# A fused transformer kernel on one core: value and output products of the first cross attention from 16-bit halves

## What is computed

```python
q = (inputs_q @ Wq).reshape(b, sq, H, HD) * (1.0 / np.sqrt(HD))
k = (inputs_kv @ Wk).reshape(b, skv, H, HD)
v = (inputs_kv @ Wv).reshape(b, skv, H, HD)
scores = jnp.einsum('bqhd,bkhd->bhqk', q, k)
attn = jax.nn.softmax(scores, axis=-1)
ctx = jnp.einsum('bhqk,bkhd->bqhd', attn, v).reshape(b, sq, H * HD)
return ctx @ Wo
```

## Time and profile before

| | |
|---|---|
| median of the runs | 704.66 us |
| the profiled execution | 703.56 us, span of its instructions 702.3 us |
| PE busy | 662.5 us (94%) |
| weight loads busy (beside PE) | 421.8 us (60%) |
| DVE busy | 557.1 us (79%) |
| ACT busy | 379.8 us (54%) |
| POOL busy | 333.7 us (48%) |
| value products (L942), 50 to 420 us | 16.0 us in 104 instructions |
| output products (L948), 50 to 420 us | 14.9 us in 50 instructions |
| last output product of the first attention (L948) | 470.3 us |

### The profile page before, as it was taken

How to read it: one execution, slowest core, us unless ns; L and a number is a source line. 1 busy time by engine, 2 the same in 40 slices (tenths; PEclk the granted TensorE clock), 3 DMA queues, 4 the chain that set the end, 5 groups by cost and what they waited for, 6 DMA issues and landing times. The chain is left out here.

```text
span 702.3 us, 13255 instructions
## 1 busy us (share of the span) xinstructions
PE 662.5 (94%) x4895; PEld 421.8 (60%) x4895; DVE 557.1 (79%) x1000; ACT 379.8 (54%) x610; POOL 333.7 (48%) x449
## 2 busy tenths in 40 slices
PE   9899999999999999999999999996999889887887
PEld 7466766667666776766766666752456444443453
DVE  5997867977787786887988667875897889988655
ACT  5643433334433353443443344445998899898841
POOL 5884444544545416569543316425645543344401
PEclk9999999999999999999999999998999999999999
DMA  9656688565556688987686965519998989998910
GB/s 313 177 125 157 153 171 182 135 150 126 136 129 136 143 181 221 195 204 165 167 182 126 201 137 131 141 39 265 187 193 156 168 156 192 158 177 152 160 37 8
DMA packets 347152, 111.23 MB, mean 158 GB/s; under 512 B 313544, under 2 KB 344528, under 8 KB 346832
## 3 DMA queue, kind: packets, MB, share of 16 engines
q1 hardware_dynamic: 347088, 110.39, 74.7%
HBM read 32.23 MB, written 0.26 MB: 46 GB/s over the span
## 5 line engine op out<-in xcount | busy, mean ns | idle before, releaser
L919 PE MATMUL psum<-c_nat,eT 128*128 128x256 f16 x1536 | 188.1, 273 | 0.9 <-ACT u_sb L1058 0.9
L1702 DVE TENSOR_REDUCE tops<-psum 128x1 f32<-128x512 f32 x256 | 159.2, 680 | 24.5 <-PE psum L1653 24.2
L1695 ACT ACTIVATE cT<-psum,bias,q_scale 128x1024 f16<-128x1024 f32 x128 | 153.5, 1205 | 26.3 <-PE psum L1653 18.4
L919 PEld LDWEIGHTS psum<-c_nat,eT 128*128 128x128 f16 x1536 | 150.3, 98 | 27.0 <-issue 1.6
L891 PE MATMUL psum<-cT,qk 128*128 128x512 f16 x744 | 165.6, 379 | 0.1
L1653 PE MATMUL psum<-kT,v_space 128*128 128x512 f16 x512 | 140.5, 383 | 15.8 <-DVE tops L1702 9.3
L891 PEld LDWEIGHTS psum<-cT,qk 128*128 128x128 f16 x744 | 72.6, 98 | 82.2 <-issue 1.0
L1096 DVE TENSOR_REDUCE neg_max<-psum 128x1 f32<-128x2048 f32 x32 | 73.3, 2290 | 30.9 <-PE psum L891 30.6
L1653 PEld LDWEIGHTS psum<-kT,v_space 128*128 128x128 f16 x512 | 44.6, 98 | 80.7 <-DVE tops L1702 41.5
L1084 DVE TENSOR_TENSOR e_lo<-e_all,e_hi 128x2048 f16<-128x2048 f32 x32 | 87.5, 2733 | 0.0
L732 ACT ACTIVATE qT<-psum 128x128 f32<-128x128 f32 x32 | 8.9, 279 | 120.4 <-PE psum L714 120.3
(11 more groups left out here) (252 smaller groups left out, 901.4 us busy)
## 6 DMA issues: line engine op xcount, KB each, us to landing
wq_h<-in_L_xattn_Wq SPq DMA_DIRECT2D x32, 128.0 KB, 2.5
wk_h<-in_wkT SPq DMA_DIRECT2D x32, 128.0 KB, 2.6
wv_h<-in_L_xattn_Wv SPq DMA_DIRECT2D x32, 128.0 KB, 2.3
wo_h<-in_L_xattn_Wo SPq DMA_DIRECT2D x32, 128.0 KB, 2.5
mx_land<-in_mx_weights SPq DMA_DIRECT2D x8, 384.0 KB, 3.5
v_space<-in_ctx SPq DMA_DIRECT2D x4, 512.0 KB, 5.7
cT<-in_ctx SPq DMA_DIRECT2D x2, 1024.0 KB, 7.6
c_nat<-in_expert_wT SPq DMA_DIRECT2D x2, 1024.0 KB, 6.4
```

The costliest lines, as they stand in the source:

```text
L919: ins = pe.matmul(u_ps, c.eT[:, v % 2, e_part, j, :], m.c_nat[:, v // H0, c_part, j, :], start=(j, e_part, c_part) == (0, 0, 0), stop=(j, ...
L1695: act.activation(m.y[:, u % 2, q * CHUNK:(q + 1) * CHUNK], m.bank(second_place(u, q), 2), ACT.Exp, bias=m.bias[:, u:u + 1], scale=m.q_scal ...
L1702: dve.tensor_reduce(m.tops[:, n // NB, n % NB:n % NB + 1], m.bank(n % 3), AX.X, ALU.max, negate=True).then_inc(s["q_max"], 1)
```

## The change

The value product reads 16-bit halves of Wv (`wvo_parts`, first half high, second low) and of the transposed u, three products per 128 rows of Wv (`TERMS`: high x high, high x low, low x high), six of 128 columns in all; the output product reads halves of the value product and of Wo, three of 256 columns (`HALVED`: for heads 0 to 28; head 29 keeps the fp32 output product). Wv and Wo of a head now lie beside each other in one tile of 512 columns with two places. ACT copies it to fp16 at the head of unit u = w+4; POOL subtracts the copy from it, right behind L672, in the same unit. The fp32 sum of the halves of u (L660) goes, and the halves have two places. ACT's copy of the value product (L1011) is now the high half, and DVE takes the low one right behind the reciprocal. SP loads the output weights behind the transposes of u, and waits for the split two units back instead of an output product. The last two heads take their weights in the places of the query weights, and their uT_sb lies in the place of qk.

```diff
--- before.py
+++ after.py
@@ -43,6 +43,7 @@
 FP8_UNIT = 2.0 ** -6
 UNITS = B * H0
 TURNED = UNITS - 2
+HALVED = TURNED - 1
 
 UP = 64.0
 E_UP = 1024.0
...
@@ -287,15 +288,16 @@
         self.eT = sb("eT", [P, 2, 2, KTB, P], FP16)
         self.wq_h = sb("wq_h", [P, 2, KD, HD0])
         self.wk_h = sb("wk_h", [P, 2, D])
-        self.wv_h = sb("wv_h", [P, 3, KD, HD0])
-        self.wo_h = sb("wo_h", [P, 3, D])
+        self.wvo_h = sb("wvo_h", [P, 2, 2 * D])
+        self.wvo_parts = sb("wvo_parts", [P, 2, 2 * D], FP16)
         self.qT = sb("qT", [P, P])
         self.qk = sb("qk", [P, 2, 2, KD, P], FP16)
         self.u_sb = sb("u_sb", [P, D])
         self.u_parts = sb("u_parts", [P, 2, D], FP16)
-        self.uT_parts = sb("uT_parts", [P, 2, KD, P], FP16)
-        self.uT_sb = sb("uT_sb", [P, 2, KD, P])
+        self.uT_parts = sb("uT_parts", [P, 2, 2, KD, P], FP16)
+        self.uT_sb = flat(self.qk).bitcast(F32).rearrange("p (a k q) -> p a k q", a=2, k=KD)
         self.oT_sb = sb("oT_sb", [P, P])
+        self.oT_parts = sb("oT_parts", [P, 2, P], FP16)
         self.v_top = sb("v_top", [P, D])
         self.neg_max = sb("neg_max", [P, 2])
         self.row_sum = sb("row_sum", [P, UNITS])
@@ -531,10 +533,19 @@
 
 
 def sp_load_output(sp, c, s, t, u):
-    h, sem = u % H0, s[f"wvo_in{u % 3}"]
-    sp.dma_start(c.wv_h[:, u % 3, :, :], t["L0_xattn_Wv"].rearrange("(k p) n -> p k n", p=P)
+
+    h = u % H0
+    if u < TURNED:
+        values, out, sem = value_weights(c.wvo_h[:, u % 2, :]), c.wvo_h[:, u % 2, D:2 * D], s[f"wvo_in{u % 2}"]
+    else:
+        values, out, sem = c.wq_h[:, u % 2, :, :], c.wk_h[:, u % 2, :], s[f"wqk_in{u % 2}"]
+    sp.dma_start(values, t["L0_xattn_Wv"].rearrange("(k p) n -> p k n", p=P)
                  [:, :, h * HD0:(h + 1) * HD0]).then_inc(sem, 16)
-    sp.dma_start(c.wo_h[:, u % 3, :], t["L0_xattn_Wo"][h * HD0:(h + 1) * HD0, :]).then_inc(sem, 16)
+    sp.dma_start(out, t["L0_xattn_Wo"][h * HD0:(h + 1) * HD0, :]).then_inc(sem, 16)
+
+
+def value_weights(both):
+    return both[:, 0:D].rearrange("p (k n) -> p k n", k=KD)
 
 
 def sp_cross(sp, m, c, d, g, s, t):
@@ -542,10 +553,6 @@
         if u + 3 < UNITS:
             sp.wait_ge(s["qk_mm"], u + 2)
             sp_load_query(sp, c, s, t, u + 3)
-        if 4 <= u <= UNITS + 1:
-            if u > 4:
-                sp.wait_ge(s["head_out"], u - 4)
-            sp_load_output(sp, c, s, t, u - 2)
         if 0 < u <= UNITS:
             v = u - 1
             if v > 1:
@@ -555,6 +562,12 @@
             sp.wait_ge(s["e_lo"], v + 1)
             sp.dma_start_transpose(c.eT[:, v % 2, 1], c.e_lo[:, :]).then_inc(s[f"lo_turned{v % 2}"], 16)
             sp_turn_values(sp, c, s, v - 2)
+        if 4 <= u <= UNITS + 1:
+            if u - 2 < TURNED:
+                sp.wait_ge(s["wvo_parts"], 2 * (u - 3))
+            else:
+                sp.wait_ge(s["qk_mm"], UNITS)
+            sp_load_output(sp, c, s, t, u - 2)
         if 0 < u <= H0:
             for kt in (2 * u - 2, 2 * u - 1):
                 sp.wait_ge(s["k_cut"], kt + 1)
@@ -607,10 +620,10 @@
 
 def sp_turn_values(sp, c, s, v):
     if 0 <= v < TURNED:
-        if v > 0:
-            sp.wait_ge(s["uT_out"], v)
+        if v > 1:
+            sp.wait_ge(s["oT"], v - 1)
         sp.wait_ge(s["u_lo"], v + 1)
-        sp.dma_start_transpose(c.uT_parts.rearrange("p a k q -> p (a k) q"), flat(c.u_parts)).then_inc(
+        sp.dma_start_transpose(c.uT_parts[:, v % 2].rearrange("p a k q -> p (a k) q"), flat(c.u_parts)).then_inc(
             s[f"u_turned{v % 2}"], 16)
 
 
@@ -652,15 +665,6 @@
                            ALU.subtract).then_inc(s["c_lo"], 1)
 
 
-def pool_turned_values(pool, c, s, w):
-    if 0 <= w < TURNED:
-        pool.wait_ge(s[f"u_turned{w % 2}"], 16 * (w // 2 + 1))
-        if w > 1:
-            pool.wait_ge(s["oT"], w - 1)
-        pool.tensor_tensor(flat(c.uT_sb[:, w % 2]), flat(c.uT_parts[:, 0]), flat(c.uT_parts[:, 1]), ALU.add).then_inc(
-            s["uT_out"], 1)
-
-
 def pool_cross(pool, m, c, d, g, s, side):
     full = d.k_full.rearrange("p (h d) -> p h d", h=H1)
     for u in range(UNITS + 3):
@@ -670,6 +674,10 @@
             if w > 0:
                 pool.wait_ge(s[f"u_turned{(w - 1) % 2}"], 16 * ((w - 1) // 2 + 1))
             pool.tensor_tensor(c.u_parts[:, 1, :], c.u_sb[:, :], c.u_parts[:, 0, :], ALU.subtract).then_inc(s["u_lo"], 1)
+        if (turned := turned_due(u)) is not None:
+            pool.wait_ge(s["wvo_parts"], 2 * turned + 1)
+            pool.tensor_tensor(c.wvo_parts[:, 1, :], c.wvo_h[:, turned % 2, :], c.wvo_parts[:, 0, :],
+                               ALU.subtract).then_inc(s["wvo_parts"], 1)
         side.upto(4 * u + 1)
         if u in (1, 2):
             tiles = slice((u - 1) * LATE, u * LATE)
@@ -689,10 +697,6 @@
             pool.tensor_tensor(hi, ints, scale, ALU.mult).then_inc(s["k_pool"], 1)
             pool.wait_ge(s["k_pool"], 2 * kt + 2)
             pool.tensor_tensor(lo, full, hi, ALU.subtract).then_inc(s["k_cut"], 1)
-            if kt % 2 == 0:
-                pool_turned_values(pool, c, s, w)
-        if u >= H0:
-            pool_turned_values(pool, c, s, w)
         side.upto(4 * u + 2)
         if H0 + 2 <= u < H0 + 2 + KT // 4:
             value_round(pool, m, s, 2 * (u - H0 - 2) + 1)
@@ -937,15 +941,38 @@
     def value_product(w):
         if w > 0:
             pe.wait_ge(s["added"], w)
-        pe.wait_ge(s[f"wvo_in{w % 3}"], 32 * (w // 3 + 1))
+        pe.wait_ge(s[f"u_turned{w % 2}"], 16 * (w // 2 + 1))
+        pe.wait_ge(s["wvo_parts"], 2 * w + 2)
         for k in range(KD):
-            ins = pe.matmul(o_ps[:, D:D + P], c.wv_h[:, w % 3, k, :], c.uT_sb[:, w % 2, k, :], start=k == 0,
+            for w_part, u_part in TERMS:
+                ins = pe.matmul(o_ps[:, D:D + P], value_weights(c.wvo_parts[:, w_part, :])[:, k, :],
+                                c.uT_parts[:, w % 2, u_part, k, :], start=(k, w_part, u_part) == (0, 0, 0),
+                                stop=(k, w_part, u_part) == (KD - 1, 1, 0))
+        ins.then_inc(s["oT"], 1)
+
+    def output_product(w):
+        pe.wait_ge(s["oT_out"], w + 1)
+        if w < HALVED:
+            pe.wait_ge(s["oT_lo"], w + 1)
+            for o_part, w_part in TERMS:
+                ins = pe.matmul(o_ps[:, 0:D], c.oT_parts[:, o_part, :], c.wvo_parts[:, w_part, D:2 * D],
+                                start=(o_part, w_part) == (0, 0), stop=(o_part, w_part) == (1, 0))
+        else:
+            ins = pe.matmul(o_ps[:, 0:D], c.oT_sb[:, :], c.wvo_h[:, w % 2, D:2 * D], start=True, stop=True)
+        ins.then_inc(s["head_out"], 1)
+
+    def last_value_product(w):
+        pe.wait_ge(s["uT_copied"], w - TURNED + 1)
+        pe.wait_ge(s["added"], w)
+        pe.wait_ge(s[f"wqk_in{w % 2}"], 32 * (w // 2 + 2))
+        for k in range(KD):
+            ins = pe.matmul(o_ps[:, D:D + P], c.wq_h[:, w % 2, k, :], c.uT_sb[:, w % 2, k, :], start=k == 0,
                             stop=k == KD - 1)
         ins.then_inc(s["oT"], 1)
 
-    def output_product(w):
+    def last_output_product(w):
         pe.wait_ge(s["oT_out"], w + 1)
-        pe.matmul(o_ps[:, 0:D], c.oT_sb[:, :], c.wo_h[:, w % 3, :], start=True, stop=True).then_inc(s["head_out"], 1)
+        pe.matmul(o_ps[:, 0:D], c.oT_sb[:, :], c.wk_h[:, w % 2, :], start=True, stop=True).then_inc(s["head_out"], 1)
 
     for u in range(UNITS + 3):
         v = u - 2
@@ -966,7 +993,6 @@
         side.upto(4 * u + 1)
         w, last = turned_due(u), last_due(u)
         if w is not None:
-            pe.wait_ge(s["uT_out"], w + 1)
             value_product(w)
             if last is not None:
                 output_product(w)
@@ -983,8 +1009,7 @@
         drain(u, 2)
         side.upto(4 * u + 3)
         if last is not None:
-            pe.wait_ge(s["uT_copied"], last - TURNED + 1)
-            value_product(last)
+            last_value_product(last)
         elif w is not None:
             output_product(w)
         if u < H0:
@@ -998,7 +1023,7 @@
             ins.then_inc(s["v_scale_pe"], 1)
         drain(u, 3)
         if last is not None:
-            output_product(last)
+            last_output_product(last)
 
 
 def act_cross(act, m, c, s, side):
@@ -1008,7 +1033,7 @@
         act.wait_ge(s["oT"], w + 1)
         if w > 0:
             act.wait_ge(s["head_out"], w)
-        act.copy(c.oT_sb[:, :], o_ps[:, D:D + P]).then_inc(s["oT_out"], 1)
+        act.copy(c.oT_parts[:, 0, :] if w < HALVED else c.oT_sb[:, :], o_ps[:, D:D + P]).then_inc(s["oT_out"], 1)
 
     for u in range(UNITS + 3):
         v, w, last = u - 2, turned_due(u), last_due(u)
@@ -1016,6 +1041,11 @@
             tiles = slice((u - 1) * LATE, u * LATE)
             act.wait_ge(s[f"late_in{u - 1}"], 16)
             act.copy(m.c_nat[:, 1, 0, tiles, :], c.late_land[:, tiles, :]).then_inc(s["late_hi"], 1)
+        if w is not None:
+            act.wait_ge(s[f"wvo_in{w % 2}"], 32 * (w // 2 + 1))
+            if w > 0:
```

(18 more changed lines are left out.)

1 line of the change is left out of this document (removed).

## The result

The changed kernel takes 727.34 us (median of 4 runs, 725.28 to 727.93), the kernel before, measured beside it, 704.32 (4 runs, 703.86 to 705.30): a ratio of 1.032, 95% interval 1.0296 to 1.0343. It is **slower by 3.2%**. The forecast was 722 us with a range of 704 to 731. The profiled execution of the changed kernel took 725.28 us (span 723.9), 21.7 more than that of before (703.56). The median of the runs stands 2.1 higher; what it may be made of comes with the fourth experiment.

A forecast was written before the change was run, and what follows sets the result against it. TensorE was taken as full from 50 to 420 us; -6.6 + 4.8 + 0.6 + 17.2 + 2.0 = +18.0 on 703.56 gave 721.6, with the median 1.1 higher 722.6, taken as 722 us, range 704 to 731.

The forecast's parts named there:

- products, 0.22 a unit: TensorE's value products save 3.5 us in 30 heads, output products 3.1 in 29: -6.6 us.
- heads 1, 5, 9: Units with the long reduction: value products wait 1.28, 1.73 and 1.78 us for GpSimd's subtraction, +4.8 us.
- head 12: Value product with lead 0.85 us and no key tile ahead of it: +0.6 us.
- half clock: After head 28's wait, about 4 us of TensorE at the 1.2 GHz level: +2.0 us.
- Rival (d): Weight loads don't hide under the value product's six 128-column products: 727 to 732 us; chance 0.05.
- The lead: GpSimd's L672 must end 1.43 us before the value product: 1.16 subtraction, about 0.05 semaphore, 0.22 earlier PE.
- rival (c): Half clock after heads 16, 26 and 28, and a subtraction overlapping e_lo as L672 did: 728 us; chance 0.10.
- VectorE's remainder: Waiting for ScalarE's copy, it starts key tile 2u 1.41 us later; 2.04 us of idle absorbs this in ordinary units.
- The second half: GpSimd's slice rounding and side stages stand ahead of L672, so heads there wait for the split: +17.2 us together.
- rival (a): Odd units 19 to 31: GpSimd runs ahead without L660's 61.8 us of waiting, 698.1 to 703.5 us; chance 0.17.
- Rival (b): Only heads with negative leads wait, VectorE absorbs its wait: 707 us, or 711 with the full 1.43; chance 0.15.
- What cost nothing: ScalarE's weights copy costed at nothing (18 us if uncovered); SyncE's moved loads hidden, otherwise 1 us per long unit.

The follow-up runs named there:

- experiment 4: Changed kernel with 14, 13 and 20 idle PE products of 512 columns ahead of its waits for heads 16, 26 and 28: 722.69 us.
- Experiment 3: Changed kernel with VectorE's remainder of the value product behind key tile 2u instead of ahead of it: 723.85 us.
- Experiments 2 and 5: Both edit the changed kernel: the first does the weights' split one unit earlier, 700.86 us; the second swaps GpSimd's two subtractions, 721.02 us.
- experiment 7: Changed kernel, split one unit earlier, VectorE's remainder behind the key tile and, in the second half, also behind odd units' slice work: 709.42 us.

## Why the prediction was right, and where its sizes were off

The forecast case was what happened. For the profiled executions it said +18.0 us; it was +21.7. That the total came so near is in part luck: the waits were 2.0 us less than forecast (20.6 for 22.6), and what came on top of them 5.6 more. The sign and the place do not rest on it: PE's list has nine waits of 19.0 us for the weights, where I expected some 11 of 22. Term by term:

| | forecast | measured |
|---|---|---|
| products, 0.22 a unit | -6.6 | -6.4 |
| heads 1, 5, 9 | 1.28, 1.73, 1.78 | 1.29, 1.73, 1.76 |
| head 12 | 0.6 | 0.4 |
| heads 14, 16, 17, 20 | 0.1, 4.6, 0.9, 0.3 | 0.2, 3.9, 0, 0.5 |
| heads 22, 26, 28 | 2.4, 3.9, 5.0 | 2.0, 3.5, 5.3 |
| half clock | 2.0 | 4.6 |
| elsewhere | 0 | 3.0 |
| sum | +18.0 | +21.7 |

A head's measured figure is how much later its value product starts than that of before, by more than the head ahead of it did, and 0.22 on top for the product's saving (head 28 less the 0.31 by which the side wait in its unit grew).

- **Products.** The six of the value product take 0.33 us, as the earlier trace rows gave. Rival (d), weight loads that show, is out. The sustained pace that the Trainium skill gives (TensorE: Matmul & The Clock Gate, Back-to-back issue gap), about 81 ns, is not what this trace shows for six products in a row between products of 256 columns: 55 ns.
- **The lead.** The subtraction took 1.15 us against my 1.16 interpolated from L672 and L651, and the hand-over with the semaphore 0.1 (300.54 less 300.40 is 0.14). No L679 overlapped its way to 2 us, as rival (c) had it (1147 to 1157 ns in all 30); L676 ahead of it did, as before.
- **VectorE's remainder.** It waited 1.46 us for ScalarE's copy in head 5's unit and took 0.29; key tile 2u then began 1.04 us behind the value product (145.85, 144.81) where it had begun 0.36 ahead of it (128.01 in the earlier trace rows, 128.37 in the earlier trace rows), 1.40 later as worked out; and the 2.04 us of idle before add_output shrank to 0.41. Experiment 3 shows the 3.5 us that this costs.
- **The second half.** Heads 16, 22, 26 and 28 are the long ones, as worked out. GpSimd's freed time did not bring its queue forward at head 16 (L445 waited 7.32 us for VectorE's rstd, the gate that the forecast named), so rival (a) is out. Rival (b), only the negative leads, is out by the waits of heads 1, 5, 9 and 22. Head 17 had none, where 0.9 was forecast: its value product came with 1.65 us to L676's end, where before it was 0.52, since PE ran at half speed between the two heads; in experiment 4, without that stretch, head 17 waits 0.18. Head 16 was 0.7 less late than forecast; the forecast named SP's earlier e_hi transposes as a possible gain of half a microsecond, and the trace shows the place, though not as named. Ahead of the rstd that gates GpSimd, ScalarE's fp16 copy of the exponentials waited for the last transpose of e_hi before the change and no longer does:

```profile
286.29 1.90 ACT L1036 CAST e_hi<-e_all 128x2048 f16<-128x2048 f32 x1 [0.67 <-DMA eT<-e_hi]
...
287.73 1.90 ACT L1066 CAST e_hi<-e_all 128x2048 f16<-128x2048 f32 x1
```

That transpose was issued 0.7 us later against PE than before, not earlier (at 279.82 and 277.05, where the score products of that unit of PE start at 277.74 and 275.67), but landed 7.4 us after its issue instead of 9.2. Why it was quicker was not tried.
- **The failed term: the clock.** I took one stretch at the 1.2 GHz level, after head 28, on the pattern of the earlier trace rows, at 2.0 us, and left heads 16 and 26 to the range. The clock fell at all three, for 3.41 us each, and cost 1.6, 1.3 and 1.7 us. I had no ground for treating waits of 4.6 and 3.9 us otherwise than one of 5; the trace of before had only the one of 5.16. Experiment 4 confirms the size. The fourth stretch, after head 22, would, if my reading holds, be in the median and not in the profile, and make 1.65 of the 2.1 us between them.
- **Elsewhere**, which the forecast had at nothing: some 1.8 us among the side products (0.3 at head 13, 1.3 at heads 24 and 25, of which PE's two waits at L490 make 0.8, and 0.3 at head 28, where L1640's wait is 0.76 for 0.45), and 1.4 at the handover, where the wait is 6.79 us for 5.16.
- **What cost nothing** did so: ScalarE's copy of the weights took 0.61 us and PE waited for it nowhere; no wait for SP's moved loads or for the kT transposes appears among PE's.

The forecast's chance of 0.80 for slower rested on the reading that PE was full and GpSimd's lead over it was thinner than the new work. Experiments 2 and 5 are the proof: the same work, a unit or 0.63 us earlier, and the loss goes in whole or in part.

## What to carry to other kernels

When an engine with idle time is given work that the full engine waits for, its idle share says nothing: take, head by head, the distance between the last thing it does before and the moment its result is needed, and subtract the new work. If the distance is shorter anywhere, give the work a place one unit earlier, with a second buffer for its result, before anything is made faster. And look at both ends of an operation that you move: what stands behind its wait, and who waits for its result; experiment 7 lost 8.6 us by looking at the first only.
